# Preparation of a four-layer graph network: edge rows first, one histogram in place of two, in-degrees from an extra column of the first product

## The chip, the cores and the metric

The kernel runs on one core of a Trainium2 chip. The metric is the time of one execution on the device, in microseconds (us): median 3203.28 of 3 runs, from 3202.03 to 3203.89. The engines are TensorE (PE in the profile, its weight loads PEld), VectorE (DVE), ScalarE (ACT), GpSimd (POOL) and SyncE (SP), which here only issues DMAs. An engine works through its instructions in the order in which they are written; a semaphore wait holds all that stands behind it.

## The reference

A graph of N = 3125 nodes with D = 128 features and E = 50000 edges, each with 64 attributes; the edges are sorted by destination. Four layers, each added to its input, each behind a layer norm and a ReLU:

```python
h = max(layernorm(x), 0); x = x + GCN(h)          # this layer and what prepares it are changed
h = max(layernorm(x), 0); x = x + Transformer(h)  # 8 heads, edge attributes, softmax by destination, FFN
h = max(layernorm(x), 0); x = x + GAT(GAT(h))     # 3 heads, then 1
h = max(layernorm(x), 0); x = x + SAGE(SAGE(h))   # mean over incoming edges

# GCN
norm_out = rsqrt(max(deg_out, 1)); norm_in = rsqrt(max(deg_in, 1))
h2  = (h * norm_out) @ W
agg = segment_sum(h2[src], dst)
y   = agg * norm_in + b
out = relu(layernorm(y) * gamma + beta) + h
```

deg_out counts the edges that leave a node (the source histogram), deg_in those that enter it. In-degrees are also wanted for the first and last edge of each node (the places where the attention layers scatter their sums) and for the mean in SAGE.

## The kernel before

**Tiles.** The nodes are 25 tiles of 128 (NT = 25). The edges are 391 blocks of 128 which are padded to CH = 392 and taken in NG = 98 groups of four blocks. Nodes are also counted in 782 groups of DG = 4. The GCN sum is made as a dense product. An edge block and a node group that touch make a "step"; there are some 1,172 steps, ten chunks (NC) of 128. For each step a 100 x 128 piece of a matrix "adj" holds how often source (key: tile and place in it) meets destination (in the group of four). It is made by one-hot products in NB = 147 batches of eight steps. Then adj (100 pieces of 128 x 128 in a chunk) is multiplied with the scaled node features, and 40 such results, "v rows", are sorted to their nodes by a last product ("pick").

**The head (prep).** Almost all of it hangs in one chain on the semaphore `s_steps`: a step waits until the counter has reached its number. SP issues all loads (`load`, L565): weights, `x_sb`, and copies of src and dst into padded lists `esrc` and `edst` in HBM; it waits for all of them, and then loads the edge rows `src_r`, `dst_r`, `prev_r` from those lists. DVE compares `dst_r` and `prev_r` (L1605, are the edges sorted?), makes floats, PE turns them, and DVE splits them into low seven bits and the rest (`lo_f`, `hi_f`). The step search (L1697 compare of 3,910 elements, L1700 sum over them, L1704) gives the step's block index, by which POOL gathers the steps' edges with 20 indirect DMAs (L853, L856). Beside these DVE writes one-hots for two histograms, source and destination, in 49 turns of eight blocks each (`hot`, L1706 to L1720), and PE multiplies them (L1237 on). Behind them stand the keys (L1723 to L1735), the degrees and the chain of index steps for each node's first and last edge (L1738 to L1810), the boundary rows (PE L1257), the 16 weight transposes and the column products (L1267), batch-norm rows, the transposes of the keys (L1275), and the layer norm of x with the split of h times norm into three bf16 parts, `xs0` (chain "n0", L1839 to L1860), each step over 3,200 elements, on DVE and ACT in turns. ACT's queue issues the reversed copy of the edge attributes (49,920 rows of 64 floats, "fill", L951 and L953) and then the zeros for the scatter targets `starts` (L959): seven parts of 3.6 MB each and two more.

**The loop over NB batches.** DVE writes one-hots `hot_e` and `hot_k` (`hot_steps`, L1868 and L1870) and, two times in three batches, a `same` mask (L1878), which needs a destination row from SP (`load_dst_row`, L642). PE makes eight products of 100 columns (L1301), ACT copies them into adj (L1002), and behind every fourth batch PE makes one `spmm`: 25 products of 384 columns against `xs0` (L1290). SP stores each `same` mask (`store_same`), loads the row four groups ahead, and stores each finished adj chunk (`store_adj`). DVE sums the three parts of each v row (`v_row`, L1882). Since `spmm` runs one chunk behind, eight of its 40 pieces stand behind the loop.

**The tail.** DVE writes the selection matrix `sel` (L1887), PE makes 112 pick products (L1319) in 8 banks, and DVE and ACT copy the banks out.

```python
1284  pe.wait_ge(adj_done, min(NB, (ch + 1) * PER))
1285  if n == 0:
1286      pe.wait_ge(s_steps, chains["n0"].end)
```

Of the kernel before, what the change touches and what calls it, by code (L numbers as in the profile page):

```python
# [13 lines left out]
P = 128  # L14
# [38 lines left out]
PIECES = NT // HI  # L53
RING = 9
# [96 lines left out]
def gnn_stack_kernel(nc, out, x, src, dst, edge_attr_64, **w):  # L151
    ctx = ExitStack()
    with ctx:
# [40 lines left out]
        deg = sb("deg", [P, 2, NT])  # L194
        norm = sb("norm", [P, 2, NT])
# [71 lines left out]
        def place(at, parts, *dims):  # L267
# [51 lines left out]
        xs0 = carve(arena, {"xs": (P, (NT, 3, D), BF16)}, adj_v)["xs"]  # L319
        vrow_at = adj_v + NT * 3 * D // 2  # L320
# [8 lines left out]
        n0_t = carve(arena, {"n0_t": (P, (NT, D), F32)}, 8000)["n0_t"]  # L329
# [7 lines left out]
        hists = carve(arena, {"hot_lo": (P, (4, P, BATCH), BF16), "hot_hi": (P, (4, NT, BATCH), BF16)}, hist_at)  # L337
# [11 lines left out]
        sel_early = carve(arena, {"sel": (P, (SPAN_AT[NC],), F32)}, work_at)["sel"]  # L349
# [5 lines left out]
                     | {"dst_fl": (H1, (2, CH), F32), "part_i": (P, (CH,), I32),  # L355
                        "lo_f": (P, (2, CH), BF16), "hi_f": (P, (2, CH), BF16), "raw": (P, (16, D), F32)})
# [25 lines left out]
        s_steps = sem("s_steps")  # L382
        s_hot = sem("s_hot")
# [52 lines left out]
        FILLS = 16 * 2  # L436
        ZEROS = 16 * (7 + 1 + 1)
        s_sort_dve, s_sort_pool, s_sort_dma = sem("s_sort_dve"), sem("s_sort_pool"), sem("s_sort_dma")
        s_seed = sem("s_seed")
# [3 lines left out]
        pe_o, act_o, dve_o, pool_o = (Order(sem(f"node_{e}")) for e in ("pe", "act", "dve", "pool"))  # L443
        pe_o.lay("gcn", ("lin", 0), ("tr", 3), ("qkv", 3))
# [32 lines left out]
        def chain(key, names, turns=1):  # L477
# [3 lines left out]
        wt = [f"wt{i}" for i in range(16)]  # L481
        chain("prep", ["consts", "pads", "pads_out", "edges_in", "look_lt", "look_sum", "look_ps", "look_i",
                       "sort_in", "sort_hist", "sort_pre", "sort_pre_sb", "sort_tot", "sort_rank", "sort_move", "iota_f", "cast", "brk", "brk2",
                       "cols", "cols_i", "bits", "bits_f"])
        chain("hist", ["hist_start", "hist_read", "deg_max", "deg_sqrt", "deg_norm", "cnt_r", "cum_ps", "tot_sb", "tot_scan",
                       "tot_ex", "cum", "nz", "end", "end_ii", "end_xor", "end_f", "end_m", "end_i",
                       "blk_i", "blk_f", "start", "inner", "blk_m", "blk_n", "gi_m", "gi",
                       "st_i", "st_x", "st_f", "id_f", "st_d", "st_m", "st_n", "start_i",
                       "bnd_ps", "last_sb", "link", "cont", "pen",
                       "wt_ps", "wt_sb", "bn_var", "bn_sd", "bn_rs", "bn_a", "bn_b1", "bn_b2", "bn_b3", "brk_out"])  # L490
        chain("n0", ["mean", "neg", "cent", "sq", "var", "vare", "sd", "rs", "hs", "hn", "hi", "r1", "mid", "r2", "lo"])
        for p in ("gcn",) + PASSES + ("sage1", "sage2"):
            if p in WEIGHTED:
                chain("s_" + p, ["firsts"] + (["er_in", "er_ps", "er_sb"] if p != "attn" else []))
                chain("x_" + p, ["z_in", "r_out"])

# [20 lines left out]
        def part(ap, t):  # L517

            return ap[:, t * P:(t + 1) * P]

# [40 lines left out]
        def _(sp):  # L561
# [9 lines left out]
            c = chains["prep"]  # L571
# [17 lines left out]
            load(raw[:, 0:3, :], w["L2_gnn_fc1_w"].rearrange("(h p) n -> p h n", p=P))  # L589
            load(raw[:, 3:6, :], w["L2_gnn_res1_w"].rearrange("(h p) n -> p h n", p=P))  # L590
            load(raw[:, 6:9, :], w["L2_gnn_fc2_w"].rearrange("p (h n) -> p h n", h=H2))
            load(raw[:, 9:12, :], w["L2_gnn_res2_w"].rearrange("p (h n) -> p h n", h=H2))
            for i, k in enumerate(("Wl0", "Wr0", "Wl1", "Wr1")):
                load(raw[:, 12 + i, :], w[f"L3_gnn_{k}"])
            with nc.allow_non_contiguous_dma(reason="attention vectors as columns"):
                for i, k in enumerate(("attn_l", "attn_r")):
                    load(a1[:, i, :], w[f"L2_gnn_{k}1"].rearrange("h p -> p h"))
                    load(a2[:, i:i + 1], w[f"L2_gnn_{k}2"].rearrange("h p -> p h"))
            full = N // P * P
            load(x_sb[:, 0:NT - 1, :], x[0:full, :].rearrange("(t p) n -> p t n", p=P))  # L600

            sp.wait_ge(s_setup, 1)
            load(x_sb[0:N - full, NT - 1, :], x[full:N, :])

            load(esrc[0:E].rearrange("(a n) -> a n", a=16), src.rearrange("(a n) -> a n", a=16))
            load(edst[P:P + E].rearrange("(a n) -> a n", a=16), dst.rearrange("(a n) -> a n", a=16))
            sp.wait_ge(s_steps, c.at("pads_out"))
            load(edst[0:P].rearrange("(p a) -> p a", a=1), pad_i[:, 0:1])
            npad = EP - E
# [54 lines left out]
            for g in range(NG):  # L664
                store_same(g)
                if g + UNROLL < NG:
                    load_dst_row(g + UNROLL)
# [1601 lines left out]
```

## Time and profile before

| what | us |
|---|---|
| median of 3 runs (lowest, highest) | 3203.28 (3202.03, 3203.89) |
| the profiled execution, its span | 3204.94, 3203.3 |
| busy: PE, PEld, DVE | 2465.8, 1827.5, 1435.8 |
| busy: ACT, POOL | 902.1, 1358.5 |
| first `same` mask (L1878), the loop's start | 255.81 |
| last 200 products of L1290 start; picks start | 666.08; 700.91 |

The profile is of one execution on the hardware. The span goes from its first instruction to its last; the execution's own time is 1.6 us longer. A busy share over the whole span says little here, since the stages differ: the head is read in stretches of time, in the chain of waits (followed back from the last instruction, each step to what released it) and in single instructions in order of time. The head and the loop together are the first 724 us of 3203; the stages behind the picks are not touched but for where a few waits stand.

### The profile page before, as it was taken

To read this page: it belongs to the slowest core of one execution; us is meant where nothing else is said; L and a number is where in the kernel's file an instruction comes from. 1 tells how busy PE (TensorE), PEld (TensorE's weight loads), DVE (VectorE), ACT (ScalarE), POOL (GpSimd) and SP (SyncE) were. 2 spreads that over 40 slices of the span, in tenths; PEclk is the share of its full clock that TensorE was granted. 3 is DMA by queue.
4 is the path that set the end of the run, shared out by engine and by line. 5 is a ranking of instruction groups with operands and counts; after the bars stand their busy time and mean duration, and the time that the engine had idled before them with its cause. 6 is when DMAs were issued, how large, how long until landed. Compare 5 with 4: busy or idle time off the path is not lost.

```text
span 3203.3 us, 37305 instructions
## 1 busy us (share of the span) xinstructions
PE 2465.8 (77%) x12918; PEld 1827.5 (57%) x12918; DVE 1435.8 (45%) x3060; ACT 902.1 (28%) x1851; POOL 1358.5 (42%) x1414
## 2 busy tenths in 40 slices
PE   0728999995688888765888888575777776599998
PEld 0615666663577777544555555244777776266666
DVE  2947555526577776542444444332222222511313
ACT  0014222214233333254444444132222222200201
POOL 0300000005777777345777777135777775300000
PEclk9986777797898988776899999686555555699999
DMA  6934444422899999411677877322556554464461
GB/s 161 328 106 156 173 152 148 167 99 64 231 267 262 261 262 264 137 29 36 208 234 230 256 241 231 101 54 67 133 133 133 133 133 105 155 200 154 123 200 34
DMA packets 519059, 525.19 MB, mean 164 GB/s; under 512 B 153816, under 2 KB 463458, under 8 KB 517562
## 3 DMA queue, kind: packets, MB, share of 16 engines
q1 hardware_dynamic: 237144, 237.22, 24.6%
q10 hardware_dynamic: 231201, 170.37, 17.4%
q0 software_dynamic: 50528, 115.22, 14.6%
q8 instruction: 106, 1.74, 0.2%
q14 instruction: 80, 0.65, 0.1%
HBM read 306.05 MB, written 229.79 MB: 167 GB/s over the span
## 4 chain that ended last, share of the span: by engine, by line
PE 35%; POOL 31%; issue 13%; DVE 7%; DMA 6%; ACTq 4%; ACT 4%; SPq 1%; POOLq 0%; DVEq 0%
POOL arena L913 29%; PE ps L1338 10%; PE ps L1290 7%; PE ps L1301 7%; DMA arena<-t_gat,src_i 3%; ACTq L959 2%; PE ps L1319 2%; ACTq L953 1%; DMA arena<-t_attn,src_i 1%; ACT arena L944 1%; SPq L565 1%; PE ps L1534 1%; DVE arena L1998 1%; PE ps L1511 1%; PE ps L1411 1%
## 5 line engine op out<-in xcount | busy, mean ns | idle before, releaser
L944 ACT ACTIVATE arena<-ps 128x544 f32<-128x544 f32 (+8 forms) x589 | 480.7, 825 | 1600.2 <-PE ps L1411 594.1
L913 POOL DMA_INDIRECT arena<-t_gat,src_i x784 | 740.9, 945 | 238.9 <-issue 233.8
L1411 PE MATMUL ps<-arena 128*128 128x136 f32 (+2 forms) x2352 | 649.8, 436 | 111.8 <-ACT arena L944 71.6
L1411 PEld LDWEIGHTS ps<-arena 128*128 128x128 f32 x2352 | 445.7, 252 | 243.9 <-issue 85.2
L913 POOL DMA_INDIRECT arena<-t_attn,src_i x392 | 382.8, 977 | 119.5 <-issue 114.6
L1338 PE MATMUL ps<-arena 128*128 128x384 bf16 x2000 | 332.3, 330 | 35.1 <-DVE rec L2140 35.1
L1387 PEld LDWEIGHTS ps<-arena 128*128 128x128 f32 x1568 | 287.1, 267 | 35.7 <-issue 7.5
L1338 PEld LDWEIGHTS ps<-arena 128*128 128x128 bf16 x2000 | 197.6, 99 | 169.7 <-issue 43.4
L878 POOL TENSOR_TENSOR arena<-arena,r_L_gnn_gamma 128x512 f32<-128x512 f32 (+1 forms) x7 | 8.0, 1149 | 637.7 <-ACT arena L1107 637.7
L1387 PE MATMUL ps<-arena 128*128 128x3 f32 (+1 forms) x1568 | 267.0, 293 | 5.2 <-ACT arena L944 4.2
L1946 DVE TENSOR_TENSOR z_b<-arena,ps 128x12 f32<-128x12 f32 (+1 forms) x196 | 30.9, 157 | 514.2 <-DMA arena<-t_gat,src_i 460.4
L1301 PE MATMUL ps<-arena 128*128 128x100 bf16 x1176 | 222.6, 364 | 44.9 <-DVE arena L1870 44.9
L1290 PE MATMUL ps<-arena 128*128 128x384 bf16 x1000 | 232.6, 407 | 0.0
L1998 DVE TENSOR_TENSOR arena<-arena,ps 128x1536 f32<-128x1536 f32 (+1 forms) x196 | 229.9, 1215 | 5.8 <-ACT arena L1044 5.8
L1301 PEld LDWEIGHTS ps<-arena 128*128 128x128 bf16 x1176 | 170.4, 146 | 91.7 <-issue 45.3
L1290 PEld LDWEIGHTS ps<-arena 128*128 128x128 bf16 x1000 | 120.0, 120 | 106.9 <-issue 69.3
L1936 DVE TENSOR_TENSOR arena<-arena,ps 128x1024 f32<-128x1024 f32 x98 | 119.3, 1218 | 136.5 <-DMA arena<-t_attn,src_i 107.7
L1395 PE MATMUL ps<-ident,logit 128*64 128x128 f32 (+2 forms) x147 | 47.3, 322 | 172.3 <-DVE logit L1959 110.3
L944 ACT ACTIVATE arena<-same_b 128x512 f32<-128x512 bf16 x294 | 167.8, 620 | 25.8 <-DMA same_b<-same_hbm 25.8
L2224 DVE TENSOR_REDUCE arena<-ps 128x128 f32<-128x384 f32 x80 | 39.0, 550 | 274.3 <-PE ps L1338 274.3
L1395 PEld LDWEIGHTS ps<-ident,logit 128*64 128x64 f32 (+2 forms) x147 | 19.7, 134 | 182.7 <-DVE logit L1959 114.8
L1371 PE MATMUL ps<-w_e,arena 64*128 64x128 f32 x784 | 121.6, 299 | 2.7 <-DVE arena L1936 2.7
(301 smaller groups left out, 2990.7 us busy)
## 6 DMA issues: line engine op xcount, KB each, us to landing
ends_gat<-arena ACTq DMA_DIRECT2D x98, 774.0 KB, 4.9
arena<-adj_hbm SPq DMA_DIRECT2D x100, 640.0 KB, 3.9
same_b<-same_hbm SPq DMA_DIRECT2D x294, 128.0 KB
adj_hbm<-arena SPq DMA_DIRECT2D x10, 3200.0 KB, 11.2
ends_attn<-arena ACTq DMA_DIRECT2D x98, 272.0 KB, 4.9
ends_gat<-arena ACTq DMA_DIRECT2D x98, 258.0 KB, 4.6
starts_q<-zrow ACTq DMA_DIRECT2D x7, 3584.0 KB, 25.5
arena<-edst SPq DMA_DIRECT2D x98, 256.0 KB, 3.8
```

What stands on the lines that cost most here:

```text
L913: g.indirect_dma_start(out=row_b[:, n % RB, k, 0:row_tab[p].shape[1]], out_offset=None, in_=row_tab[p], in_offset=bass.IndirectOffsetOnAxi ...
L944: return a.activation(o, i, ACT.Copy)
L959: act.dma_start(flat[b].rearrange("p (a n) -> p a n", n=wide), zrow[:, 0:wide].rearrange("p (a n) -> p a n", a=1).to_broadcast([P, n // wi ...
L1290: i = mm(bank(4 + n % 4)[:, 0:3 * D], adj[:, ch % 2, t * DG + dl, :], xs0[:, t, :, :].rearrange("p s c -> p (s c)"), start=t == 0, stop=t ...
L1301: i = mm(ps[:, at:at + KEYS], hot_e[:, b % 3, :, e], hot_k[:, b % 3, :, e], start=True, stop=True)
L1338: m = mm(bank(ch % 2 * 4 + dl)[:, 0:3 * D], ring[:, u % RING, (t * DG + dl) * P:(t * DG + dl + 1) * P], xs1[:, h, :, :].rearrange("p s c - ...
L1371: i = mm(bank((1, 6)[g % 2])[:, k * D:(k + 1) * D], at_t[:, g % 2, k * P:(k + 1) * P], w_e[:, :], start=True, stop=True)
L1387: i = mm(ps[:, at:at + n_er], same_f[:, g % RB, k, :], er_c[:, g * GC + k, 0:n_er], start=True, stop=True)
L1395: nc.tensor.transpose(bank(2)[0:kh, 0:P], logit[:, i % 2, 0:kh], ident[:, :])\
L1411: i = mm(o, same_f[:, g % RB, k, :], msg[:, g % 4, k * W:(k + 1) * W], start=True, stop=True)
L1936: tt(kv, kv, bc(bank((1, 6)[g % 2]).rearrange("p (k s c) -> p k s c", k=GC, s=1), [P, GC, 2, D]), ALU.add).then_inc(kve_done.sem, 1)
L1998: tt(m[:, :, 0:heads * nc_].rearrange("p k (h c) -> p k h c", h=heads), rows_v, e, ALU.mult).then_inc(msg_done.sem, 1)
```

## The change

What it does, by engine:

- **Order of loads.** SP first loads `dst_r` and `prev_r` straight from the input in HBM (8 DMAs), then the padded lists (7), the weights to be turned (12), then all others (36) and last the fill (4). ACT's queue loads `src_r` (3) and `x_sb` (2). In place of waits for all loads there are semaphores for each kind. The rows' padding is written first, by DVE (`s_ends`).
- **Zeros.** They move from ACT's queue into SP's loop: 28 parts, one at every second group from group 10, and one each for the two GAT targets.
- **Histogram.** Only sources are counted, in 25 turns of WIDE = 16 blocks, with one instruction for 16 blocks in place of two for eight. The one-hots have a fourth dimension in their access patterns.
- **Step search.** The compare and the sum over 3,910 elements become ten instructions, one a chunk, which compare and accumulate.
- **In-degrees.** `xs0` gets a column of ones (XW = 386, 385 are used), so each `spmm` also gives the edges that a v row holds. DVE casts that column (`vdeg`), PE multiplies it with a bf16 copy of `sel` (`degrees`), and 25 products with one column turn the sums into node order (`in_degrees`). Index steps, sums and norms that need them stand on DVE and PE behind the loop, between the picks.
- **Layer norm and split.** The layer norm goes to ACT (three times 25 activations of 128 x 128). The product with the norm goes to POOL (`by_node`), as does the first subtraction (`rest`), seven turns each; ACT copies `hi` and `mid` behind its first 14 evictions, and DVE subtracts `lowest` in the loop at batches 4, 6, ..., 16, straight into `xs0`.
- **Small chains.** Breaks, boundary rows, batch-norm rows and weight transposes get counters of their own (`own_chain`); the batch-norm rows go into the loop.

```diff
+XW = 3 * D + 2
+FULL = E // P
+WIDE = 2 * BATCH
+HTURNS = -(-CH // WIDE)
+DEG_LATE = NC - 1
@@ SP
-            load(x_sb[:, 0:NT - 1, :], x[0:full, :].rearrange("(t p) n -> p t n", p=P))
...
-            landed()
-            sp.sem_inc(s_steps, 1)
-            sp.wait_ge(s_steps, c.at("edges_in"))
-            load(src_r[:, :, :], esrc.rearrange("(a t e) -> t a e", a=QA, e=P))
-            load(dst_r[:, :, :], edst[P:P + EP].rearrange("(a t e) -> t a e", a=QA, e=P))
+            fill(eattr[0:FULL * P, :].rearrange("(t p) c -> t p c", p=P),
+                 edge_attr_64[0:FULL * P, :].rearrange("(t p) c -> t p c", p=P)[:, ::-1, :])
...
-            sp.wait_ge(s_steps, chains["n0"].end)
+            sp.wait_ge(step_idx, 1)
+            sp.wait_ge(s_edges, EDGES)
+            sp.wait_ge(s_steps, chains["prep"].end)
             for g in range(UNROLL):
                 load_dst_row(g)
...
+                if g >= 10 and g % 2 == 0 and g // 2 - 5 < ZERO_PARTS:
+                    zeros(starts["attn"], ZERO_PARTS, g // 2 - 5, 256)
@@ POOL
+            def by_node(j):
...
+                gt(tiles(hn, j), tiles(h_sb, j),
+                   bc(norm[:, 0, t0:t1].rearrange("p (k c) -> p k c", c=1), [P, count(j), D]), ALU.mult).then_inc(pool_o.sem, 1)
+            def rest(j):
+                pool.wait_ge(act_o.sem, act_o.at("n0", "hi", j))
+                gt(tiles(hn, j), tiles(hn, j), split_of(j, 0), ALU.subtract).then_inc(pool_o.sem, 1)
@@ ACT
+            for t in range(NT):
+                i = a.activation(h_sb[:, t, :], x_sb[:, t, :], ACT.Copy, accum_out=total[:, t:t + 1])
...
+                if b < len(act_o.seq["n0"]):
+                    step, j = act_o.seq["n0"][b]
+                    (hi if step == "hi" else mid)(j)
@@ DVE
-            tt(cmp[:, :, :], bc(val_f[:, 0:CH - 1].rearrange("p (a b) -> p a b", a=1), [P, NC, CH - 1]),
-               bc(step_f[:, 0, :].rearrange("p (c a) -> p c a", a=1), [P, NC, CH - 1]), ALU.is_le).then_inc(step_cmp, 1)
+            for ch in range(NC):
+                i = stt(cmp[:, ch, :], val_f[:, 0:CH - 1], step_f[:, 0, ch:ch + 1], zrow[:, 0:CH - 1], ALU.is_le, ALU.add,
+                        accum_out=step_f[:, 1, ch:ch + 1])
...
-                    tt(hot_lo[:, 2 * slot + s, :, :], iota_rep[:, :, :],
-                       bc(lo_f[:, s, cols].rearrange("p (a k) -> p a k", a=1), [P, P, BATCH]), ALU.is_equal)
+                for o, parts, k in ((hot_lo, P, lo_f), (hot_hi, NT, hi_f)):
+                    i = tt(o[:, slot, :, 0:r * BATCH].rearrange("p i (a k) -> p i a k", a=r),
+                           bc(iota_rep[:, 0:parts, :].rearrange("p i (a k) -> p i a k", a=1), [P, parts, r, BATCH]),
+                           bc(k[:, at:at + r * BATCH].rearrange("p (i a k) -> p i a k", i=1, a=r), [P, parts, r, BATCH]),
+                           ALU.is_equal)
...
+            def lowest(j):
+                dve.wait_ge(act_o.sem, act_o.at("n0", "mid", j))
+                tt(split_of(j, 2), tiles(hn, j), split_of(j, 1), ALU.subtract).then_inc(dve_o.sem, 1)
...
+            in_loop = {2 * j + 4: (lowest, j) for j in range(NJ)}
...
             def v_row(n):
                 dve.wait_ge(spmm_done, n + 1)
+                v.tensor_copy(vdeg[:, n // DG, n % DG:n % DG + 1], bank(4 + n % 4)[:, 3 * D:3 * D + 1])
@@ PE
-                    i = mm(bank(4 + n % 4)[:, 0:3 * D], adj[:, ch % 2, t * DG + dl, :],
-                           xs0[:, t, :, :].rearrange("p s c -> p (s c)"), start=t == 0, stop=t == NT - 1)
+                    i = mm(bank(4 + n % 4)[:, 0:3 * D + 1], adj[:, ch % 2, t * DG + dl, :],
+                           xs0[:, t, 0:3 * D + 1], start=t == 0, stop=t == NT - 1)
...
+            def in_degrees():
+                pe.wait_ge(s_in, in_c.at("tiny"))
+                for t in range(NT):
+                    m = min(P, NGRP * DG - t * P)
+                    i = mm(bank(7)[0:m, t:t + 1], by_dl[:, :, :].rearrange("d g e -> d (g e)")[:, t * P:t * P + m],
+                           ones[0:DG, 0:1], start=True, stop=True)
+                i.then_inc(s_in, 1)
...
+                        if i == 0 and (half, dl) == (1, 0):
+                            in_degrees()
+                        if i == 0 and (half, dl) == (1, 1):
+                            in_sums()
```

The order of instructions on SP around the first destination rows (`arena<-edst`, 128 x 512), before. The rows `arena<-esrc` and the two behind it are the edge rows, `breaks` the attention's block breaks; in square brackets stands the semaphore that is waited for.

```order
L565 DMA ends_gat<-zrow 128x129
L565 DMA arena<-esrc 98x4x128 [waits s_load,s_steps]
L565 DMA arena<-edst 98x4x128 x2
L565 DMA breaks<-arena 98x4x128 [waits s_load,s_steps]
L565 DMA breaks<-arena 97x1
L565 DMA breaks<-arena 98x3x1
L565 DMA breaks<-ntmp 1x1
L646 DMA arena<-edst 128x512 [waits s_load,s_steps]
L646 DMA arena<-edst 128x512 x3
```

The same place on SP in the changed kernel (`eattr` is the list that the fill writes, `same_hbm` takes the masks):

```order
L593 DMA ends_gat<-zrow 128x387
L593 DMA ends_gat<-zrow 128x129
L669 DMA eattr<-zrow 48x64
L669 DMA eattr<-zrow 128x64
L669 DMA eattr<-in_edge_attr 2x80x32
L669 DMA eattr<-in_edge_attr 49920x1x64
L689 DMA arena<-edst 128x512 [waits s_steps,s_edges,step_idx]
L689 DMA arena<-edst 128x512 x3
L696 DMA same_hbm<-same_b 128x512 [waits same_done]
L689 DMA arena<-edst 128x512 [waits same_done]
```

The edge rows and the breaks are gone from this place, the four fill DMAs now stand directly ahead of the first destination row on the same queue, and that row no longer waits for the normalised features.

On DVE at the head of the loop, before (L1868 and L1870 are the one-hots, L1878 the `same` masks):

```order
L1868 TENSOR_TENSOR arena<-arena 128x1024 [waits built]
L1870 TENSOR_TENSOR arena<-arena 128x800
L1878 TENSOR_TENSOR same_b<-arena,dst_i 128x512 [waits dst_row_in2]
L1868 TENSOR_TENSOR arena<-arena 128x1024 [waits built]
L1870 TENSOR_TENSOR arena<-arena 128x800
L1878 TENSOR_TENSOR same_b<-arena,dst_i 128x512 [waits dst_row_in3]
```

The same place in the changed kernel, where L1940, L1942 and L1950 are those lines and L1908 is the last part of the split (`lowest`):

```order
L1940 TENSOR_TENSOR arena<-arena 128x1024 [waits built]
L1942 TENSOR_TENSOR arena<-arena 128x800
L1908 TENSOR_TENSOR arena<-arena 128x4x128 [waits node_act]
L1950 TENSOR_TENSOR same_b<-arena,dst_i 128x512 [waits dst_row_in3]
L1940 TENSOR_TENSOR arena<-arena 128x1024 [waits built]
L1942 TENSOR_TENSOR arena<-arena 128x800
L1940 TENSOR_TENSOR arena<-arena 128x1024 [waits built]
L1942 TENSOR_TENSOR arena<-arena 128x800
L1908 TENSOR_TENSOR arena<-arena 128x4x128 [waits node_act]
```

A subtraction that waits for ACT's `mid` copy now stands among the one-hots, behind every second batch from the fifth, seven in all.

On PE in the middle of the picks (L1463, before L1319) of the changed kernel; L1435 is `in_degrees`, L1441 and L1442 are the sums:

```order
L1463 MATMUL ps<-arena 128x13
L1435 MATMUL ps<-ones,arena 128x1 [waits s_in]
L1435 MATMUL ps<-ones,arena 128x1 x23
L1435 MATMUL ps<-ones,arena 56x1
L1463 MATMUL ps<-arena 128x121
```

Before, the pick of 121 columns followed that of 13 directly; now 25 products with one column stand between, behind a wait for DVE.

## Rows read from the trace of the kernel before

**Rows 1.** Busy time by stretches: start:end, length, each engine (count), clock, DMA, GB/s.

```profile
200.00:240.00 40.00, 8.69 (x52) 8.23 (x50) 22.69 (x21) 8.65 (x11) 0.00 (x0) 0.60 0.02 5
254.70:286.30 31.60, 30.26 (x161) 22.90 (x162) 31.59 (x57) 15.90 (x19) 0.00 (x0) 0.50 0.63 193
```

**Rows 2.** Chain of waits to 730 us: start us, us, what.

```profile
48.53 3.63 DMA arena<-edst
...
54.16 1.55 ACTq L951
...
55.75 47.94 ACTq L953
...
619.77 6.61 PE ps L1290 x25
...
666.08 34.11 PE ps L1290 x200
...
700.91 23.15 PE ps L1319 x112
```

**Rows 3.** Order in time, the head: start us, us, engine, line, operation, [idle <-releaser].

```profile
0.93 0.40 SPq L565 DMA_DIRECT2D r_L_gnn_b<-in_L_gnn_b  x1
...
29.10 4.04 SPq L565 DMA_DIRECT2D x_sb<-in_x  x2
...
38.94 0.91 SPq L565 DMA_DIRECT2D ends_gat<-zrow  x2
...
52.23 0.69 DVE L1605 TENSOR_TENSOR arena<-arena 98x512 f32<-98x512 int32 x1 [52.23 <-SPq L626]
...
77.51 4.23 DVE L1700 TENSOR_REDUCE step_f<-arena 128x10 f32<-128x3910 f32 x1
...
81.93 0.17 DVE L1704 TENSOR_SCALAR step_i<-step_f 128x10 int32<-128x10 f32 x1
...
157.96 0.82 DVE L1723 TENSOR_SCALAR arena<-arena 128x1280 int32<-128x1280 int32 x1
...
164.94 1.49 DVE L1735 SCALAR_TENSOR_TENSOR arena<-arena 128x1280 f32<-128x1280 f32 x1
...
206.63 2.37 PE L1275 MATMUL ps<-ident,arena 128*128 128x128 f32 x10 [2.45 <-ACT w L944]
...
255.81 0.69 DVE L1878 TENSOR_TENSOR same_b<-arena,dst_i 128x512 bf16<-128x512 int32 x1
```

**Rows 4.** Order in time, POOL's gathers of the steps' edges, first and last of 20.

```profile
82.39 1.28 POOL L853 DMA_INDIRECT arena<-esrc,step_i  x1 [77.88 <-DVE step_i L1704]
...
111.72 1.25 POOL L856 DMA_INDIRECT arena<-edst,step_i  x1 [0.30 <-issue]
```

**Rows 5.** The page's DMA issues: count, KB each, median us to landing.

```profile
adj_hbm<-arena SPq DMA_DIRECT2D x10, 3200.0 KB, 11.2
...
starts_q<-zrow ACTq DMA_DIRECT2D x7, 3584.0 KB, 25.5
arena<-edst SPq DMA_DIRECT2D x98, 256.0 KB, 3.8
```

**Rows 6.** Order in time, POOL beside DVE behind the picks.

```profile
736.10 0.16 DVE L2086 SCALAR_TENSOR_TENSOR nm<-mv,rs 128x4 f32<-128x4 f32 x1
...
738.02 1.26 POOL L878 TENSOR_TENSOR arena<-arena,r_L_gnn_gamma 128x512 f32<-128x512 f32 x1 [3.49 <-ACT arena L1107]
...
738.38 0.92 DVE L2086 SCALAR_TENSOR_TENSOR nm<-mv,rs 128x4 f32<-128x4 f32 x1
```

**Rows 7.** Order in time, short steps of the head: index chain, boundary rows, column products.

```profile
182.76 0.18 DVE L1762 TENSOR_SCALAR ntmp<-deg 128x25 f32<-128x25 f32 x1
...
187.85 1.49 PE L1257 MATMUL ps<-ident,dst_f 128*98 128x1 f32 x8 [6.03 <-DVE start_i L1810]
...
202.71 0.58 PE L1267 MATMUL ps<-a,arena 128*128 128x1 f32 x4
...
203.38 0.58 PE L1267 MATMUL ps<-a,arena 128*128 128x1 f32 x4
```

More of the change, by code:

```diff
@@ L479, in chain @@
             total[0] = chains[key].end
[L481 to L491, printed above, removed]
+        chain("prep", ["consts", "pads", "iota_f", "look_lt", "look_sum", "look_ps", "look_i",
+                       "sort_in", "sort_hist", "sort_pre", "sort_pre_sb", "sort_tot", "sort_rank", "sort_move", "cast",
+                       "cols", "cols_i"])
         for p in ("gcn",) + PASSES + ("sage1", "sage2"):
@@ L624, in _ @@
-            load(prev_r[:, :, :], edst[P - 1:P - 1 + EP].rearrange("(a t e) -> t a e", a=QA, e=P))
-            landed()
-            sp.sem_inc(s_steps, 1)
-            sp.wait_ge(s_steps, chains["hist"].at("brk_out"))
-            load(breaks[0:CH, 0:P].rearrange("(a t) e -> t a e", a=QA), brk_r[:, :, :])
-            with nc.allow_non_contiguous_dma(reason="the break that opens the next block"):
-                load(breaks[0:CQ - 1, P:P + 1], brk_r[1:CQ, 0, 0:1])
-                load(breaks[CQ - 1:CH - 1, P:P + 1].rearrange("(a t) e -> t a e", t=CQ), brk_r[:, 1:QA, 0:1])
-                load(breaks[CH - 1:CH, P:P + 1], ntmp[0:1, 8, 0:1])
@@ new lines, in _ @@
+            act.dma_start(x_sb[0:N - full, NT - 1, :], x[full:N, :]).then_inc(s_x, 16)
+            act.wait_ge(s_x, X_IN)
+            act.wait_ge(s_steps, chains["prep"].at("cast"))
+            total, less, square, dev = (t[:, 0, :] for t in (rs, nm, sd, sd))
+            for t in range(NT):
+                i = a.activation(h_sb[:, t, :], x_sb[:, t, :], ACT.Copy, accum_out=total[:, t:t + 1])
+            i.then_inc(s_ln, 1)
+            act.wait_ge(s_ln, ln_c.at("neg"))
+            a.activation(less, total, ACT.Copy, scale=-1.0 / D).then_inc(s_ln, 1)
@@ new lines, in _ @@
+            act.wait_ge(s_bits, bits_c.end)
+            act.dma_start(breaks[0:CH, 0:P].rearrange("(a t) e -> t a e", a=QA), brk_r[:, :, :]).then_inc(s_brk, 16)
+            with nc.allow_non_contiguous_dma(reason="the break that opens the next block"):
+                act.dma_start(breaks[0:CQ - 1, P:P + 1], brk_r[1:CQ, 0, 0:1]).then_inc(s_brk, 16)
+                act.dma_start(breaks[CQ - 1:CH - 1, P:P + 1].rearrange("(a t) e -> t a e", t=CQ), brk_r[:, 1:QA, 0:1])\
+                   .then_inc(s_brk, 16)
+                act.dma_start(breaks[CH - 1:CH, P:P + 1], ntmp[0:1, 8, 0:1]).then_inc(s_brk, 16)
@@ L991, in _ @@
+            act.wait_ge(s_ln, ln_c.at("h"))
+            for t in range(NT):
+                i = a.activation(h_sb[:, t, :], x_sb[:, t, :], ACT.Relu, scale=rs[:, 1, t:t + 1], bias=nm[:, 1, t:t + 1])
+            i.then_inc(s_ln, 1)
+            act.wait_ge(s_out, out_c.at("sqrt"))
+            a.activation(norm[:, 0, :], norm[:, 0, :], ACT.Sqrt).then_inc(s_out, 1)
             act.wait_ge(keys_ps, 1)
@@ new lines, in _ @@
+            dve.wait_ge(s_in, in_c.at("scan"))
+            v.tensor_tensor_scan(tot_x[:, :], ones[:, 0:NT], tot[:, :], 0.0, ALU.mult, ALU.add)
+            v.reciprocal(cnt_r[:, :], norm[:, 1, :]).then_inc(s_in, 1)
+            dve.wait_ge(s_in, in_c.at("ex"))
+            tt(tot_x[:, :], tot_x[:, :], tot[:, :], ALU.subtract).then_inc(s_in, 1)
+            dve.wait_ge(s_in, in_c.at("last"))
+            tt(cum[:, :], tot_x[:, :], cum[:, :], ALU.add).then_inc(s_in, 1)
+            dve.wait_ge(s_in, in_c.end)
```

609 lines of the change are left out of this document (343 added, 266 removed).

## The prediction, made before the changed kernel ran

> **What bounds the kernel now.** I read the busy table by stretches first, then the chain of waits, then the order in time of single instructions, and last the groups by form. The stretch 200 to 240 us shows DVE busy 22.69 of 40 us, PE 8.69 and DMA 2% [rows 1]: nothing is full, one engine waits for the next. The chain says why the stage lasts until 256 us [rows 2]: a landing at 48.5, the DMA queue of ACT blocked for 47.9 us behind the edge-attribute fill, then behind the zero writes, short DVE steps that were only held back by those, the transposed weights, the serial normalisation on DVE and ACT, and only then PE. From 256 to 700 us the chain is PE alone: pieces of 32 one-hot products, 25 products with 384 columns, and 200 of these at the end (34.11 us), followed by the 112 picks (23.15 us) [rows 2]. So the reader is to see three places: a head of some 256 us that is waits, a loop of 444 us that PE bounds, and a tail of 24 us on PE.
>
> **The head: when the loop starts.** The loop truly starts when DVE gets its first destination row, at 255.81 [rows 3] (its first one-hot needs the keys, its second item this row). Two branches end there in the new kernel, and I take the later.
>
> Branch one is SP's queue. The big fill of attributes (49,920 rows of 256 B) moves from ACT to SP, as the last of 67 DMAs, and the first row loads stand directly behind it. Before, 59 issues took from 0.93 to 39.85 us [rows 3]; without the two of x (4.04 us), which now go by ACT, that is (38.92 - 4.04)/57 = 0.612 us each, so 67 take 41.0 and the fill is issued at about 42. The fill itself took 1.55 us and held the next DMA on its queue for 47.94 us [rows 2]; nothing suggests less, since it was alone with gathers beside it then, and it is so again. Then the row load lands in 3.8 us [rows 5]. Sum: 42.0 + 1.6 + 47.9 + 3.8 = 95.3 us. From below: the row load isn't held at all by the fill, and branch two decides. From above: the fill shares the engines with more traffic, 10 us later.
>
> Branch two is DVE. The edge rows come straight from the inputs, by the 8th issue (1.0 + 8 x 0.61 = 5.9), and land 3.6 us later [rows 2]: 9.5 us in place of 52.23 [rows 3]. From there to the block indices it was 81.93 + 0.17 - 52.23 = 29.9 us [rows 3]. Out of this go the counter casts (1.3 us, an estimate from 0.4 to 0.7 us for such sizes, now before the wait), the two break operations (1.2 us), most of the eight bit operations (3.4 us) and the reduction over 3,910 elements (4.23 us) [rows 3]; ten accumulating compares over the same 3,910 elements cost what one pass over them did, and ten fixed parts: +0.6. That leaves 19.8 and indices at 29.3 us. Pool's 20 gathers start then and take 112.97 - 82.39 = 30.6 [rows 4] and some 6 to land: 66 us. DVE: 2.1 us of leftovers, then one histogram in place of two: 98 pairs took 157.96 - 82.0 = 76 us, 0.775 a pair [rows 3]; 49 pairs' worth is 38, less the fixed parts of 24 pairs in the wide form: 36, and 3 us of waiting for PE, which stands in the weight transposes. That is 70, the key arithmetic 8.9 more (164.94 is its last instruction, 157.96 its first) [rows 3], 20 transposes at 2.37 us for ten, one key copy 1.2: 84 us. ACT's layer norm has from 15 to 50 us, the middle of the histogram, for 50 activations of 128x128, 0.7 us each, before it is late; the other small chains (breaks, batch-norm rows, boundary rows) lie beside it or in the loop. So DVE has 11 us of cover, SP's branch decides, and the loop starts 255.8 - 95.3 = **160.5 us earlier**.
>
> **The loop.** What was the serial split of 40 us now stands inside: Pool scales and subtracts (14 instructions), ACT copies (14, one behind each of its first 14 evictions), DVE subtracts 7 times. Until its first 384-column product this stretch has DVE busy 31.59 of 31.60 us, and PE ran at 0.50 of the clock, the lower level, 1.2 GHz [rows 1]: DVE is its bound. Seven subtractions of 128x512 at 0.60 us: +4.2 us. Pool's instructions would only run beside DVE if they left it alone. They may not: DVE's offset multiply takes 0.16 us alone and 0.92 us when issued 0.36 us into a Pool multiply of 1.26 us, and it ends at 739.30 where Pool's ends at 739.28 [rows 6]. Four of Pool's 14 fall before 95 us, while DVE waits for the row anyway; 10 x 1.26 = 12.6 us. From below 0 (they find the gaps between DVE's instructions, as when Pool was the one that waited), from above 14 x 1.26 = 17.6; I take 12.6. If they don't hold DVE up, a Pool step of 1.26 us still lies under a batch's 1.5 us (DVE's 31.59 us for some 21 batches).
> The Trainium skill (SBUF — State Buffer, "SBUF: two separate sides") says that Pool and a DVE instruction with two SBUF inputs take a shared port pair as an exclusive lock, held for the whole instruction. The trace agrees in the two rows named; by that rule the stretch costs 12.6 to 17.6 us, without it 4.2 us in all.
>
> The zero writes (25.7 MB) are cut in 28 and put on SP in the loop, one every second group. Seven parts of 3,584 KB landed in 25.5 us (median) behind each other [rows 5]. Behind a zero part and an adjacency store (11.2 us) a row load lands 14.2 + 3.8 = 18 us after its issue [rows 5] and is wanted four groups, 18 us, later. Close, five to eight times: from 0 to 30 us, I take 2 because DVE is idle half of the time there. One more column of 384 is 1000 x 0.4 to 0.8 ns, under 1 us: 1. A dense piece of 25 takes up to 6.61 us where the end of the loop has 34.11/8 = 4.26 [rows 2]; how PE's clock falls into step with the new loop may be worth 5 us in either direction, which I leave in the range.
>
> **The tail.** On the path come: 13 bf16 products of 3,144 columns in all for the degrees before the last 25 (dense rate 34.11 us/200 for 384 columns is 0.44 ns a column: 1.4 us, with fixed parts 2.0), one more DVE cast 0.1; 25 float products with a single column: the like ones take 203.38 - 202.71 = 0.67 us for three (two of this line and one beside them) [rows 7], so 5.6, and 9.3 by the slower row (1.49 us for four); I take 5.6, its weights being 128 wide too. Two sums, 1.0. The chain of 23 index steps on DVE, from 182.76 to PE's start behind it at 187.85, 5.1 us [rows 7], and eight others (2.2 us) run while PE makes three picks of 23.15/8 = 2.9 us; DVE's copies behind it come 0.7 us late. The 25 thin products may let PE's clock fall before the last picks; the dense piece above lost 2.4 us to that, so 0 to 4, take 2. Sum 2.0 + 0.1 + 5.6 + 1.0 + 0.7 + 2.0 = **11.4 us**, from 8 to 19. Nothing behind the tail changes.
>
> **The sum.** The profiled execution took 3204.94 us (span 3203.3 and 1.6 around it). 3204.9 - 160.5 + 4.2 + 12.6 + 2 + 1 + 11.4 = 3075.6; the median of the runs shown, 3203.28, lies 1.7 lower: **3074 us**.
>
> **Rivals.** (a) Pool doesn't hold DVE up and the fill is issued and drained some us sooner: -12.6 - 5: 3056. For it: Pool also waited for DVE at times; against: [rows 6]. (b) The wide one-hot form with four dimensions runs at one element a cycle, not at the narrow form's rate: +33 us of histogram, 117 us, 22 past the fill: 3096. Against it: inner runs of 8 elements and types are as before. (c) Row loads behind zero parts and adjacency stores come late, about 1.2 us for each of 28 parts: 3108. For it: the margin above is nil. (d) Slower than before: SP becomes the loop's bound. A zero part lands in a quarter of 25.5, 6.4 us, two rows 2 x 3.8, two stores 2 x 2.3: 18.6 us if one waits for the other, where PE takes 9 for two groups: 28 x 9.6 = 269 us, 3343. It decides against the change once a part costs over 129/28 = 4.6 us. Against: the queue held several transfers at once before.
>
> **How the numbers follow.** Forecast 0.58 (its own range 3062 to 3090), (a) 0.18, (b) 0.08, (c) 0.13, (d) 0.03. The range takes in (a) and (b) and most of (c): 3048 to 3112. Within 0.2% (6 us, about what a measurement of this kernel can tell) of before could only be a mild (d): 0.01. Faster 0.96, slower 0.03.
>
> **What would show it.** The first row load on SP issued near 91 us with the fill before it; the DVE one-hots of the loop at 84 us, and a wait for a DMA behind the first. A wide histogram instruction at 1.1 to 1.2 us (2.2 means b). DVE instructions in the first 25 us of the loop stretched to 1.3 us and more, beside Pool. PE busy without gaps from there for about 425 us (waits for destination rows mean c). 25 thin products in 5 to 6 us after half of the picks. Wrong is the forecast above all if the fill doesn't hold back the rows behind it, or holds them longer.

## The result and the profile after

The changed kernel takes 3070.61 us (median of 4 runs, 3066.96 to 3078.56) where the kernel before takes 3203.56; the ratio is 0.9589, interval 0.957 to 0.9608. The forecast was 3074. The profiled execution is the slowest of the four (3078.56, span 3076.9), so the account below is made against 3203.3 - 3076.9 = 126.4 us, of which the head gives more and the rest takes some back.

| stretch | before | after | difference | forecast |
|---|---|---|---|---|
| start of the loop (first destination mask) | 255.81 | 102.55 | -153.3 | -160.5 |
| from there to the first wide product | 30.5 | 42.5 | +12.1 | +16.8 |
| from there to the last run of wide products | 379.8 | 380.7 | +0.9 | +3 |
| from there to the first product behind the picks | 58.9 | 72.1 | +13.2 | +11.4 |
| all behind | 2478.3 | 2479.0 | +0.7 | 0 |

The chain of waits of the changed kernel, around the loop's start and in the tail (start us, us, what), answers to [rows 2]:

```profile
32.94 18.48 DVE arena L1854 x26
51.86 15.55 DVE arena L1854 x22
...
83.53 1.46 DVE arena L1940
85.48 17.05 another core or an unknown queue
...
127.51 6.86 POOL arena L940
...
145.08 6.55 PE ps L1392 x25
...
525.78 30.42 PE ps L1392 x175
556.20 1.48 PE ps L1413 x13
557.68 4.25 PE ps L1392 x25
562.81 11.61 PE ps L1463 x56
574.42 8.57 PE ps L1435 x50
582.99 4.90 PE ps L1463 x14
```

DVE is the path through the histogram (L1854, 34 us) and to the loop's first one-hot at 83.53. Then comes a hole of 17.05 us, which the chain can't name. The order in time does, in the rows that answer to [rows 3] (start us, us, engine, line, operation, idle before and its releaser):

```profile
47.53 1.68 SPq L669 DMA_DIRECT2D eattr<-in_edge_attr  x2
49.34 50.30 SPq L689 DMA_DIRECT2D arena<-edst  x1
...
99.69 1.37 SPq L689 DMA_DIRECT2D arena<-edst  x3
...
102.55 0.69 DVE L1950 TENSOR_TENSOR same_b<-arena,dst_i 128x512 bf16<-128x512 int32 x1 [17.08 <-DMA arena<-edst]
```

SP issues the fill at 47.53 and then stands for 50.30 us before the first destination row; DVE waits 17.08 us for that row. This is the branch that the prediction took, 7 us later than it said.

### The profile page after: what moved, and what is told of

It reads as the page before. It is cut to its first block, busy times and chain, and to the rows that moved or that the text cites. A ratio compares the mean times of both kernels' runs of the same rounds, so it can differ in the third digit from the quotient of the medians.

```text
span 3076.9 us, 36766 instructions
## 1 busy us (share of the span) xinstructions
PE 2452.4 (80%) x12590; PEld 1815.5 (59%) x12590; DVE 1385.4 (45%) x2986; ACT 927.9 (30%) x1990; POOL 1383.1 (45%) x1430
## 3 DMA queue, kind: packets, MB, share of 16 engines
q0 software_dynamic: 50528, 115.22, 14.9%
## 4 chain that ended last, share of the span: by engine, by line
PE 36%; POOL 32%; issue 13%; DVE 9%; DMA 5%; ACT 4%; another core or an unknown queue 1%; SPq 0%; POOLq 0%; PEldq 0%; DVEq 0%; ACTq 0%
POOL arena L999 30%; PE ps L1482 10%; PE ps L1392 7%; PE ps L1403 6%; PE ps L1463 2%; DMA arena<-t_gat,src_i 2%; DMA arena<-t_attn,src_i 2%; PE ps L1555 1%; PE ps L1679 1%; DVE arena L2157 1%; ACT arena L1030 1%; DVE arena L1854 1%; PE ps L1588 1%; PE ps L1718 1%; DVE arena L2095 1%
## 5 line engine op out<-in xcount | busy, mean ns | idle before, releaser
L1482 PE MATMUL ps<-arena 128*128 128x384 bf16 x2000 | 331.8, 330 | 35.2 <-DVE rec L2299 35.2
L1392 PE MATMUL ps<-arena 128*128 128x385 bf16 x1000 | 234.4, 408 | 0.0
## 6 DMA issues: line engine op xcount, KB each, us to landing
adj_hbm<-arena SPq DMA_DIRECT2D x10, 3200.0 KB, 11.8
```

The source lines that it names most:

```text
L1392: i = mm(bank(4 + n % 4)[:, 0:3 * D + 1], adj[:, ch % 2, t * DG + dl, :], xs0[:, t, 0:3 * D + 1], start=t == 0, stop=t == NT - 1)
L1482: m = mm(bank(ch % 2 * 4 + dl)[:, 0:3 * D], ring[:, u % RING, (t * DG + dl) * P:(t * DG + dl + 1) * P], xs1[:, h, :, :].rearrange("p s c - ...
```

## The experiments

The first four kernels ran in a set in which the kernel before itself took 3785.16 us, the others in sets with 3203.19 and 3206.07; each is read inside its own set or as a ratio, and where two sets are compared it is said. Behind the picks, where no edit reaches, the profiles of the later sets take 2471 to 2482 us and those of the first set 3052 to 3056; so differences ahead of the picks are read from the profiles, not from the medians.

**The changed kernel again.** No edit.

> The changed kernel once more, as the base of its neighbours and to see where its spread (3067 to 3079 us) sits. Theory fill: the loop start is set by how long the fill holds SP's queue, so where the time differs from the first profile (3078.56, first destination-row mask at 102.55 us) the mask comes earlier by as much; 3070, start 95 to 103. Rival: the spread is in the gather stages behind 660 us; then the start is 102 to 103 again and the time 3067 to 3079 all the same.

Measured: 3653.4 us, ratio 0.9654 (0.9618 to 0.9691). Neither expectation holds. The mask came at 103.20, and the queue held for 50.43 us as before, but now DVE's own keys came 18 us later (first one-hot at 101.33). The order in time of DVE in the histogram, and of POOL beside it:

```profile
45.78 1.50 DVE L1854 TENSOR_TENSOR arena<-arena 128x2048 bf16<-128x2048 bf16 x2 [4.45 <-remote]
46.20 1.63 POOL L921 DMA_INDIRECT arena<-edst,step_i  x1 [0.30 <-issue]
...
51.66 1.50 DVE L1854 TENSOR_TENSOR arena<-arena 128x2048 bf16<-128x2048 bf16 x2 [4.38 <-remote]
51.87 1.84 POOL L921 DMA_INDIRECT arena<-edst,step_i  x1 [0.30 <-issue]
```

While POOL issues its gathers (to 61.9 us) DVE makes one pair of one-hots and then stands for some 4.4 us, though nothing that it waits for is late by the profile; POOL's gather is long only where DVE gets its turn. In the first profile of the same kernel DVE had no such gap. So the two branches of the prediction both ended near 101 to 103 us here, and the 11 us of cover were gone.

That POOL's gathers hold DVE here is argued from this alternation and not shown. In this execution PE stands, too, between products for which the profile shows no wait, in a later stage with many gathers. One line of PE, in the first profile and in this one (count, then busy us, mean ns, idle us before it and its releaser):

```profile
L1515 PE MATMUL ps<-w_e,arena 64*128 64x128 f32 x784 | 123.1, 301 | 1.8 <-DVE arena L2095 1.6
```

```profile
L1515 PE MATMUL ps<-w_e,arena 64*128 64x128 f32 x784 | 146.4, 324 | 49.3 <-issue 49.1
```

Something that also reaches PE slowed the engines in this set. What it is stays open, and with it the cause of DVE's gaps.

**The fill on ACT's queue.**

```diff
- SP:  four fill DMAs ahead of the destination rows
+ ACT: four fill DMAs behind the loads of x; break stores behind the layer norm
```

> The four fill DMAs go to ACT's queue, behind the loads of x, and the break stores behind the layer norm, so no fill stands ahead of SP's destination rows. Theory fill: the first mask then follows the first one-hot at once, at 85 to 87 us in place of 102.6, less 2 us because two more of Pool's multiplies lose the cover of that wait: 14 to 16 us below the changed kernel, 3055. Rival: the fill now lies beside POOL's gathers and the weight loads and makes those late, so DVE's branch comes later by what the queue's branch gains: 3068 to 3072. Second rival: rows land late because the DMA engines are full, whatever queue they are on: same time.

Measured: 3664.1 us, 10.7 slower than the changed kernel in its set; the mask came at 109.42 in place of 103.20. SP's rows were issued at 61.72, so the queue was free as meant. But the fill now held ACT's queue, and with it ACT:

```profile
80.20 19.67 ACTq L1075 DMA_DIRECT2D breaks<-arena  x1
```

The first break store stands from 80.20 to 99.87, the square root of the norm behind it starts at 102.33, and DVE had gaps of 21.0 us in the histogram (15.9 in the run above). The edit moved the block to another engine that was on the path. It says nothing for or against the rows; the next form does.

**The fill on ACT, the breaks on SP.**

```diff
+ ACT: four fill DMAs behind the loads of x
+ SP:  four break stores ahead of the destination rows (nothing of ACT's stands behind the fill)
```

> The fill on ACT's queue behind the loads of x, and the four break stores on SP ahead of the destination rows, so that nothing but the fill stands on ACT's queue until the edge stages, and SP's rows are free by 68 us. Where DVE is not held in the histogram (keys ready at 83.5 us, as in the first profile) the loop starts at 85.5 in place of 102.6: ratio to the kernel before 0.954 (3055 of 3203). Where DVE is held beside POOL's gathers (keys at 101.3, as in the second set of runs), the queue and DVE come due together and the move gains 1 us at most: ratio 0.965 there. Rival: the earlier fill slows the loads and the gathers by what the row gains, same time on both.

Measured: 3060.4 us, ratio 0.956 (0.9544 to 0.9576), near the first case. The loop starts at once:

```profile
83.30 1.46 DVE L1941 TENSOR_TENSOR arena<-arena 128x1024 bf16<-128x1024 bf16 x1 [1.80 <-ACT arena L1027]
84.68 0.56 DVE L1943 TENSOR_TENSOR arena<-arena 128x800 bf16<-128x800 bf16 x1
85.16 0.68 DVE L1951 TENSOR_TENSOR same_b<-arena,dst_i 128x512 bf16<-128x512 int32 x1
```

85.16 in place of 102.55, and the first product behind the picks at 581.71 in place of 597.91: 16.2 us. The medians, of different sets, differ by 10; the two profiles differ by 23.9, of which 7.7 lie behind the picks (2471.3 against 2479.0). That the fill's hold of SP's queue set the start of the loop is shown.

**The fill in order.**

```diff
-  eattr[0:FULL*P] as (t p) c -> t p c  <-  the same, p reversed     # 49,920 rows of 256 B
+  eattr[0:FULL*P] as (a n) c -> a (n c), a = 128  <-  the same      # 128 rows of 99,840 B
```

> The changed kernel with the big fill at its place on SP, but copied in order, as 128 rows of 99,840 bytes in place of 49,920 rows of 256 (the reversal inside each block is left out, so the edge attributes are at wrong places). The fill held SP for 50.3 us, 12.8 MB at 254 GB/s. Theory packets: the hold comes from the number of short packets; it falls under 35 us, DVE's keys decide and the loop starts at 85: some 16 us less, 3055. Rival bytes: the hold is the bytes over the engines' rate; at the 330 GB/s that the head shows at most it is 39 us, loop at 91: 3060, or nothing changes: 3070.

Measured: 3085.72 us, ratio 0.9633 where the changed kernel has 0.9589, slower. The hold went, as the first theory has it, but neither side's loop start came: the mask stood at 109.54. SP wasn't held at all, and DVE's keys waited for POOL's gathers (order in time):

```profile
48.46 2.28 SPq L689 DMA_DIRECT2D arena<-edst  x4
...
60.00 1.11 POOL L921 DMA_INDIRECT arena<-edst,step_i  x1 [0.31 <-issue]
...
93.24 0.83 DVE L1875 TENSOR_SCALAR arena<-arena 128x1280 int32<-128x1280 int32 x1 [24.83 <-DMA arena<-edst,step_i]
```

So the hold doesn't come from the bytes. The edit changes the number of rows and drops the reversal together, so this run alone doesn't tell these two apart. The kernel before speaks for the number: its seven zero writes reverse nothing and have 3,584 rows of 1 KB each, and between 105.23 and 166.08 the next write on ACT's queue stood for 7.5 to 11.9 us each time. The gathers were issued by 61.1 us as ever, but landed only at 93, when the fill with its long rows was through; beside the fill of short rows they had landed by 69. The Trainium skill (DMA: Bandwidth & Descriptors, "Queues, rings and completion order") says that an engine takes a whole packet of one queue before it turns to the next; if longer rows make longer packets, the other queues wait longer for their turn, which is an inference. These two runs agree in direction and give no size for it.

**POOL made small.** POOL's 14 instructions act on one column of each tile; the normed features are left out so.

```diff
- gt(tiles(hn, j), ..., ALU.mult) / gt(tiles(hn, j), ..., ALU.subtract)
+ the same on [:, :, 0:1]
```

> POOL's 14 multiplies and subtractions at the head of the loop act on one column of each tile only (the normed features are left out so). Theory port: POOL and DVE hold each other up there, which cost 12.1 - 4.2 = 7.9 us between the loop start and the first 385-column product; all of it goes: 3062. As the prediction priced it (12.6): 3058. Rival: the 12.1 us are ACT's 14 copies and DVE's 7 subtractions, and POOL costs nothing: 3069 to 3071.

Measured: 3646.58 us, 6.8 below the changed kernel in its set (ratio 0.9623, 0.9584 to 0.9663, against 0.9654: the intervals overlap, so the size is taken from the profiles). From the loop's start to the first wide product, the changed kernel of that set and this one (start:end, length, busy of PE, PEld, DVE, ACT, POOL, clock, DMA share, GB/s; the answer to the second of [rows 1]):

```profile
103.20:146.85 43.65, 32.11 (x161) 22.11 (x162) 41.96 (x63) 22.45 (x33) 18.05 (x12) 0.50 0.46 138
```

```profile
104.15:139.86 35.71, 31.68 (x161) 22.27 (x162) 34.52 (x63) 22.38 (x33) 12.16 (x12) 0.50 0.55 162
```

The same 63 DVE instructions take 41.96 and 34.52 us. POOL cost 7.9 us there. In the first profile of the changed kernel the parts can be read: eight DVE instructions beside POOL are stretched by 6.0 us together (to as much as 1.62 us from 0.68), and DVE waits 1.7 us for a copy of ACT behind a subtraction of POOL that was itself held.

**The norm product on ACT.**

```diff
- POOL: hn = h * norm, seven tensor_tensor
+ ACT:  hn = activation(h, Copy, scale=norm), 25 of 128x128 ahead of the loop
```

> The product with the norm moves from POOL to ACT, as 25 activations of 128x128 ahead of the loop (7.5 us, in the stretch from 83.5 us in which the queue holds the loop anyway); POOL keeps seven subtractions. Theory port: half of POOL's turns beside DVE go, some 4 us: 3066. Rival, as above: no gain, 3069 to 3071; if ACT's products end behind the first eviction, up to 3 us slower.

Measured: 3652.47 us, 0.9 below; the stretch took 148.12 - 105.50 = 42.6 us in place of 43.65, but the first wide product came 1.3 us later (148.12 against 146.85). Inconclusive: the cover that it counted on, DVE's wait for the row, wasn't there in this set.

**Both moves.** The norm product in turns, two of seven ahead of the loop and the rest behind every second eviction; the fill as above.

> The fill on ACT and the breaks on SP as before, and the product with the norm on ACT in turns: two of seven ahead of the loop, the others behind every second eviction; POOL keeps its seven subtractions. Theories queue and port together: 17 us from the start of the loop where DVE isn't held, and 4 us from the head of the loop: ratio 0.952 to 0.953; where DVE is held 0.964. Rival: ACT, with up to 2.0 us a batch, becomes the bound of the first 20 batches and gives the 4 us back.

Measured: 3056.31 us, ratio 0.9548 (0.9532 to 0.9564), a little above the 0.952 to 0.953 expected. The stretch, without and with this move:

```profile
85.16:128.80 43.64, 32.13 (x161) 22.12 (x161) 41.96 (x63) 22.47 (x33) 18.03 (x12) 0.51 0.82 218
```

```profile
84.41:124.53 40.12, 32.13 (x161) 22.14 (x162) 38.16 (x63) 28.16 (x55) 9.72 (x7) 0.51 0.89 241
```

Half of POOL's work gone gives 3.5 us of the 7.9, close to half, and ACT doesn't become the bound. Between the medians 4.1 us, of the same set.

**The histogram late.** DVE waits for all gathers before its first one-hot.

> DVE starts the histogram's one-hots only when all 20 gathers of POOL have landed. Theory port: DVE's gaps of 3 to 15 us in the histogram come from POOL's gathers (it is held while POOL writes their descriptors); then the late histogram runs without any gap, 24 wide turns in 34 us, from some 66 to 100 us, and the loop starts at 116. Rival: the gaps come from late instruction loads or from the DMA engines, which the fill keeps full until 100 us; then the gaps stay, though the gathers are over, and the histogram takes 50 us. In time: 10 to 14 us slower than the changed kernel by the first, 25 and more by the second.

Measured: 3088.47 us, 18 above the changed kernel's median (another set; 11 between the profiles) where 10 to 14 were expected. The wait took 29.7 us, the histogram ran without a gap and the mask came at 114.99, 12.4 later, as the first theory says. But no kernel of this set had gaps, so what made them in the first set isn't told apart by it.

**The histogram narrow**, on the kernel with the fill on ACT.

```diff
- 25 turns: one-hots of 16 blocks in an instruction, [P, 16] as [2, 8]
+ 49 pairs: one-hots of 8 blocks in an instruction
```

> The kernel with the fill on ACT and the breaks on SP, with the histogram's one-hots for 8 blocks an instruction in place of 16. There DVE's branch sets the loop start, so the width shows: a wide turn takes 1.41 us, two narrow pairs 2 x 0.775, so 24.5 x 0.14 = 3.4 us later start, 88.6 in place of 85.2, and 3064 in time (ratio 0.957). Rival: the wide form with four dimensions costs as much an element as the narrow one and the fixed parts overlap: no change, start at 85.

Measured: 3087.14 us, ratio 0.9626 (0.9596 to 0.9655) where it was 0.956 without the edit (another set): some 20 us slower, not 3.4. The mask came at 109.60 in place of 85.16. The one-hots cost what was said (967 ns a pair in busy time, against 1585 a wide turn, which holds twice the blocks). Something else came (order in time):

```profile
35.88 17.45 DVE L1856 TENSOR_TENSOR arena<-arena 128x1024 bf16<-128x1024 bf16 x44
38.50 15.65 POOL L918 DMA_INDIRECT arena<-edst,step_i  x1 [0.30 <-issue]
...
53.25 0.30 DVE L1866 RECIPROCAL rs<-sd 128x25 f32<-128x25 f32 x1
53.69 4.68 DVE L1856 TENSOR_TENSOR arena<-arena 128x1024 bf16<-128x1024 bf16 x11
54.45 0.95 POOL L915 DMA_INDIRECT arena<-esrc,step_i  x1 [0.30 <-issue]
...
57.10 15.70 POOL L915 DMA_INDIRECT arena<-esrc,step_i  x1 [0.30 <-issue]
...
93.90 0.83 DVE L1876 TENSOR_SCALAR arena<-arena 128x1280 int32<-128x1280 int32 x1 [20.54 <-DMA arena<-edst,step_i]
```

Now POOL is the one held: one gather takes 15.65 us, until DVE stops for the two small steps of the layer norm at 53.25, and another takes 15.70 until the histogram ends. The last gather is issued at 88, and DVE's keys wait 20.5 us for it. The Trainium skill (SBUF — State Buffer, "SBUF: two separate sides") describes a hold of this kind for one case: while DVE runs an instruction in a 2-port perf mode, POOL is locked out of the port pair that they share and can't write the descriptors of its DMAs. The trace agrees only in the direction: the profile doesn't say in which mode these compares run, and the first gather is held not through one instruction but through some 19 pairs of them (38.50 to 53.25). A gather takes 0.94 us alone, 1.11 beside the wide one-hots of the changed kernel and 15.65 here. What decides how long it is held stays open: the kernel before used these narrow one-hots beside its gathers, and there a gather took at most 1.28 us [rows 4], 0.3 more than alone, and DVE's pairs followed each other without a gap.

**Zeros at every group** from 10 to 37, in place of every second.

> The 28 zero parts stand behind 28 groups in a row (groups 10 to 37) in place of every second one. Theory: a part costs the destination rows nothing because a row is asked for four groups (18 us) ahead: 3068 to 3073. Rival, the prediction's (c) and (d): transfers queue up behind each other; part 6.2, row 4.2 and store 2 us make 12.4 us a group where PE takes 4.5, 28 x 7.9 = 221 us more if nothing overlaps, 20 to 60 if they do by half.

Measured: 3074.82 us, ratio 0.9591 (0.9574 to 0.9608), the changed kernel's. The stretch from the first wide product to the last run is 380.8 us. Behind the first row DVE waited twice for one, 2.75 us together (once, 1.49 us, in the changed kernel), and PE lost nothing by it. So transfers on a queue overlap, and what the rows are late by is hidden, since DVE isn't the bound behind the first wide product.

**The thin products twice.**

```diff
-  for t in range(NT):
+  for t in [*range(NT)] * 2:
```

> The 25 thin products of the in-degrees are made twice. They stand on PE's path (8.6 us in the profile, 5.6 in the prediction), and the clock behind them was 0.59 for one bank of picks. Theory: 8.6 us more, and nothing more for the clock, as it had fallen already: 3079 where the changed kernel takes 3070.6. By the prediction's rate: 5.6 us more. Rival: DVE's chain of index steps behind them hides a part: under 3 us.

Measured: 3084.04 us, 13.4 above the changed kernel's median (another set); by the profiles, the first product behind the picks came 10.7 us later (608.62 against 597.91). The granted clock goes with it. Picks, thin products and next picks of the changed kernel, then of this one, then of the late histogram (columns as above):

```profile
562.70:574.40 11.70, 11.70 (x58) 8.94 (x58) 3.47 (x2) 2.62 (x3) 0.00 (x0) 1.00 0.00 0
574.40:583.00 8.60, 8.60 (x52) 8.57 (x51) 0.00 (x0) 0.85 (x1) 0.00 (x0) 0.63 0.01 2
583.00:587.90 4.90, 4.90 (x16) 3.47 (x16) 0.24 (x2) 0.00 (x0) 0.00 (x0) 0.61 0.00 0
```

```profile
574.70:593.88 19.18, 19.18 (x102) 19.12 (x101) 0.00 (x0) 0.85 (x1) 0.00 (x0) 0.56 0.00 1
```

```profile
587.20:593.36 6.16, 6.16 (x52) 6.13 (x51) 0.00 (x0) 0.85 (x1) 0.00 (x0) 0.90 0.01 3
593.36:599.10 5.74, 5.74 (x16) 4.12 (x16) 0.24 (x2) 0.00 (x0) 0.00 (x0) 0.51 0.00 0
```

25 thin products take 6.1 us where the clock holds (0.90), 8.6 where it falls within them, and 10.6 for the second 25 (19.18 less 8.6), at the lower level. The next 14 picks take 4.9 to 5.7 where a bank of them took 2.9 at full clock.

**The thin products two banks earlier**, on the kernel with both moves.

> The kernel with the fill and the norm product on ACT, and the 25 thin products and the two sums two banks of picks earlier (behind 28 picks in place of 56). Theory: PE is the bound of the tail, DVE's index chain ends before the last pick anyway; same time as without the move, 3056 (ratio 0.955), within 2 us. Rival: the index chain was on the path, or the clock recovers sooner: 3 to 5 us less.

Measured: 3054.96 us, ratio 0.9525 (0.9507 to 0.9543), the fastest. Its gain over the kernel with both moves isn't separated from nothing: 1.6 us between the profiles from the last run of wide products to the product behind the picks (70.5 and 72.1 us). In one set it is 19.9 us below the kernel with dense zeros, which is as fast as the changed kernel. So it beats both kernels.

## Why the prediction was right

Time, sign and the main mechanism were right, with each part within 8 us, and parts of the error cancelled. The forecast sum for a profiled execution was 3075.6 and the profile shows 3078.56: 7.2 us late at the start of the loop, then -4.7, -2.1, +1.8 and +0.7 in the rows of the table. That the sum misses by 3 us is in part luck, and so is that the cover on DVE's side held in the set that the forecast was measured in.

- **SP's branch, 95.3 forecast, 102.55 measured.** Right as the bound, mis-sized in two terms. "0.612 each" for 67 issues gave a fill issued by 43.6; it was 49.3. The queue stalled on the way, 4.12 us for two issues of column loads and 3.52 for one of a row: 67 issues took 0.71 us each where the 57 had taken 0.61. An issue is not of one price, and why the queue stalls at some isn't shown. The hold was 50.3 and not 47.9; 49.7 to 50.4 in the six other profiles with this fill at this place. The row landed in 2.9, not 3.8. Together +7.2.
- **DVE's branch, ready at 84, measured 83.53**, one-hots done 85.48: right, and the experiment with the fill on ACT reads it off. Its working has two slips: the 0.6 us for the fixed parts was named and not added, and the key arithmetic is 8.5 us by its rows (157.96 to 166.43), not 8.9; put right, its terms add up to 85.4, not 84. The indices came at 31.3 and not 29.3, the histogram took 35.4 and not 39. And "11 us of cover" was taken as safe. The gathers were put beside the histogram, and I gave them a price for POOL alone. In the first set DVE stood for 16 us beside them, from a cause that stays open, and in two experiments its keys waited 20.5 and 24.8 us for them.
- **POOL holds DVE, 12.6 forecast, 7.9 measured** (POOL made small). The mechanism is right, the size is not: of POOL's instructions ten lay beside DVE's, as counted, but only eight of DVE's were stretched, by 6.0 us together and not 12.6. That POOL loses too was not foreseen: one subtraction lasts 6.86 us at 127.51, while DVE works without a pause, and ACT's copy waits for it.
- **DVE's subtractions and the rest**: 12.1 - 7.9 = 4.2, the forecast value.
- **Zeros and the 385th column, 3 forecast**: 0.9. Rivals (c) and (d) are excluded, by the dense zeros too. The margin was worked out wrongly, though: its 14.2 us leave 3 for a zero part where rival (d) takes 6.4. A part landed in 6.2 us, a store in 11.8 and a row in 4.2, which is more than the 18 us of four groups, and the rows were still hardly late, since the transfers overlap.
- **The tail, 11.4 forecast, 13.2 measured.** Thin products 8.6 instead of 5.6: my rate was that of the full clock. The next picks lost 2.0 for the clock, as forecast. Degrees 1.5 (2.0), sums 0.5 (1.0), the 385th column 0.6 in the last runs, DVE's copies not late (0.7): the next product starts 0.93 us behind the last pick, as before (0.94).
- **Rival (b)** is excluded: the wide one-hot took 1.22 us. **Rival (a)**, no hold by POOL, too.

## What to carry to other kernels

In these runs a DMA of many short rows blocked the next DMA of its queue for up to 50 us, so put such a one on a queue behind which nothing on the path stands, and look whether the engine that issues it is on the path itself. When work is moved beside POOL's gathers, price the meeting for both DVE and POOL: a gather was held for 15.7 us here, and the keys behind it came 20 us late. Run the same program more than once before a cover of 11 us is called safe. A long row of tiny products costs twice: itself at the clock to which it falls, and the next big products.

## What the runs showed of the hardware that was not expected

- A gather issued by POOL took 0.94 us, 1.11 beside wide one-hots of DVE, and twice 15.7 beside narrow ones without a pause between them, which in the kernel before had cost it 0.3. In the first set DVE stood instead, up to 14.9 us at a time, for a reason that no run shows.
- A fill of 12.8 MB in 49,920 rows held its queue for 50 us; of 128 rows, not at all, but the gathers on POOL's queue landed some 24 us later beside it.
- Issued by 22.3 us on ACT's queue in place of 49.2 on SP's, the fill still held the queue until 99.9 us (the first form of that experiment), beside all the loads and gathers of the head.
- 25 products of one column took 6.1, 8.6 or 10.6 us at a granted clock of 0.90, 0.63 and, averaged with the first 25, 0.56.
